# A decoder layer on one core: the last expert's down product in two other PSUM banks, the one hot vectors built in halves, and the last four tiles' accumulators added by TensorE with the unit matrix

## The reference

```python
for e in range(48):                      # gathered tokens of expert e, at most 192
    g, u = split(xb[e] @ gate_up[e].T)   # 192 x 512 by 512 x 384
    out[e] = (silu(g) * u) @ down[e].T   # 192 x 192 by 192 x 512
final = zeros(2048, 512)
final[token of the row] += weight of the row * out[e][row]
x = layernorm(x + final)
```

## Time and profile before

| | |
|---|---|
| time, median of 3 runs | 929.57 us (929.04 to 931.65) |
| time of the profiled execution | 927.28 us |
| its span, first to last instruction | 925.5 us |
| TensorE busy | 853.3 us, 92% of the span |
| VectorE, ScalarE, GpSimd busy | 651.3, 403.7 and 466.3 us |
| mean granted TensorE clock | 0.984 |

### The profile page before, as it was taken

How to read it: one execution, slowest core, us unless ns; L and a number is a source line. 1 busy time by engine, 2 the same in 40 slices (tenths; PEclk the granted TensorE clock), 3 DMA queues, 4 the chain that set the end, 5 groups by cost and what they waited for, 6 DMA issues and landing times.

```text
span 925.5 us, 18712 instructions
## 1 busy us (share of the span) xinstructions
PE 853.3 (92%) x6014; PEld 722.1 (78%) x6015; DVE 651.3 (70%) x1473; ACT 403.7 (44%) x825; POOL 466.3 (50%) x444
## 2 busy tenths in 40 slices
PE   6799999999999989999999689999999999999891
PEld 4577777777777777888888588988889889888770
DVE  6756766577656765777777886768767686667876
ACT  4332333322333322323322156756666666566623
POOL 0242233333343231555545547767767777678355
PEclk9999999999999999999999899999999999999996
DMA  9551111211121017233222399999999999997874
GB/s 337 186 207 47 47 47 58 78 45 45 45 87 39 24 56 229 74 109 107 88 94 87 118 268 294 288 288 292 289 289 291 296 297 302 255 251 137 222 222 159
DMA packets 72350, 154.98 MB, mean 167 GB/s; under 512 B 9888, under 2 KB 10544, under 8 KB 71920
## 3 DMA queue, kind: packets, MB, share of 16 engines
q1 hardware_dynamic: 50240, 99.81, 33.1%
q0 software_dynamic: 22064, 54.58, 23.8%
HBM read 110.29 MB, written 44.07 MB: 167 GB/s over the span
## 4 chain that ended last, share of the span: by engine, by line
PE 73%; DVE 13%; issue 7%; ACT 3%; DMA 1%; POOL 1%; DVEq 0%; another core or an unknown queue 0%; POOLq 0%; SPq 0%; ACTq 0%
PE ps L621 25%; PE ps L1002 19%; PE ps L1015 11%; PE ps L991 3%; PE ps L726 2%; PE ps L716 2%; DVE arena L1445 2%; PE ps L688 1%; DVE arena L1384 1%; DVE arena L1378 1%; PE ps L888 1%; DVE arena L1919 1%; PE ps L802 1%; ACT o_hi L1213 1%; ACT arena L1065 1%
## 5 line engine op out<-in xcount | busy, mean ns | idle before, releaser
L2079 POOL DMA_INDIRECT y_rows<-arena,place_token x92 | 151.0, 1641 | 79.7 <-issue 51.7
L2068 POOL DMA_INDIRECT xg<-x_rows,place_token x96 | 95.6, 995 | 36.8 <-issue 27.1
L1002 PE MATMUL ps<-arena,raw 128*128 128x192 f32 x576 | 99.8, 331 | 3.1 <-issue 3.1
L1002 PEld LDWEIGHTS ps<-arena,raw 128*128 128x128 f32 x576 | 95.8, 193 | 6.1 <-issue 4.0
L621 PE MATMUL ps<-w_hi,x_hi 128*128 128x512 f32 (+1 forms) x332 | 77.5, 355 | 10.0 <-ACT arena L1065 4.7
L1002 PE MATMUL ps<-arena,mid_flat 128*128 128x192 f32 x432 | 73.6, 327 | 2.6 <-DVE arena L1808 1.3
L1941 POOL TENSOR_TENSOR arena<-arena,attn_pack 128x512 f32<-128x512 f32 x12 | 16.0, 1337 | 118.7 <-DVE arena L1396 118.7
L1002 PEld LDWEIGHTS ps<-arena,mid_flat 128*128 128x128 f32 x432 | 70.7, 190 | 5.2 <-issue 2.8
L621 PE MATMUL ps<-w_hi,x_lo 128*128 128x512 f32 (+1 forms) x332 | 74.5, 346 | 0.0
L621 PE MATMUL ps<-w_lo,x_hi 128*128 128x512 f32 (+1 forms) x332 | 73.0, 342 | 0.0
L621 PEld LDWEIGHTS ps<-w_hi,x_hi 128*128 128x128 f32 x332 | 52.4, 189 | 22.3 <-issue 9.3
(11 more groups left out here) (259 smaller groups left out, 2055.1 us busy)
## 6 DMA issues: line engine op xcount, KB each, us to landing
raw<-in_gu SPq DMA_DIRECT2D x24, 768.0 KB
mid_flat<-in_gu SPq DMA_DIRECT2D x18, 768.0 KB
raw<-in_dn SPq DMA_DIRECT2D x24, 256.0 KB
y_rows<-zero SPq DMA_DIRECT2D x20, 256.0 KB
mid_flat<-in_dn SPq DMA_DIRECT2D x18, 256.0 KB
arena<-in_gu SPq DMA_DIRECT2D x6, 768.0 KB
arena<-in_xT SPq DMA_DIRECT2D x16, 256.0 KB, 3.0
x_res<-in_x SPq DMA_DIRECT2D x16, 256.0 KB, 2.8
```

The source lines that it names most:

```text
L1002: m = pe.matmul(out, wgu[slot][:, q, part * P:(part + 1) * P], xgT[:, p, q, :], start=(q == 0), stop=(q == KC - 1))
L2068: pool.indirect_dma_start(out=xg[:, place, h, :], out_offset=None, in_=x2_d, in_offset=bass.IndirectOffsetOnAxis(ap=place_token[:, 2 * n + ...
L2079: pool.indirect_dma_start(out=y2_d if p and n < DUAL else y_d, out_offset=bass.IndirectOffsetOnAxis(ap=place_token[:, 2 * n + h:2 * n + h ...
```

## The change

**Banks.** The down product of the last expert goes to the banks CT and CT + 1 (0 and 1) instead of CY and CY + 1 (4 and 5). It then waits for c_copied (the turned tokens have been read from the banks 0 and 1) instead of for y_scaled of the expert before. `KEPT_BANKS` is turned so that the tiles 6 and 7 take the banks 0 and 1; a wait for y_scaled[0] ahead of the first kept product guards 4 and 5.

**Halves.** `one_hot_tokens(block, half)` now builds 8 tiles with one instruction. Half 0 stands where the two stood. Half 1 stands one expert later, between the low parts of h and `scale_y`; that of block 2 stands behind `keep_rows(0)`.

**The last four tiles** (`SUMMED = NT - 4 = 12`, pieces 6 to 8). VectorE's add L1916 and GpSimd's add L2110 of these tiles are gone. TensorE adds y2 and y to the bank itself, by two fp32 products with the unit matrix (`sum_of_both`), and waits for the loads of y and y2 first. `bn_stats` and the scaling on ScalarE read the bank.

```diff
-        KEPT_BANKS = (0, 1, 2, 3, 6, 7, 4, 5)
+        KEPT_BANKS = (2, 3, 6, 7, 4, 5, 0, 1)
...
-            def c_down(p, k):
+            def c_down(p, k, bank=CY):
                 pe.wait_ge(dn_split[p], k + 1)
                 pe.wait_ge(h_split, 2 * k + p + 1)
-                at_least(pe, y_scaled[1 - p], 2 * (k + p))
+                if bank == CY:
+                    at_least(pe, y_scaled[1 - p], 2 * (k + p))
+                else:
+                    pe.wait_ge(c_copied, 2 * E2)
...
-                        m = pe.matmul(ps[0:HALF, CY + h, :], lhs, rhs, start=(i == 0), stop=(i == len(parts) - 1))
+                        m = pe.matmul(ps[0:HALF, bank + h, :], lhs, rhs, start=(i == 0), stop=(i == len(parts) - 1))
...
-            c_down(1, E2 // 2 - 1)
+            c_down(1, E2 // 2 - 1, CT)
...
-            pe.wait_ge(c_copied, 2 * E2)
+            def sum_of_both(j):
+
+                q = piece_of(j)
+                pe.wait_ge(y2_in[0], 4 * NT)
+                pe.wait_ge(y2_in[1], 4 * NT)
+                pe.wait_ge(y_in[q % 3], 16 * (q // 3 + 1))
+                pe.matmul(ps[:, KEPT_BANKS[j % 8], :], eye, y2_all[:, j, :], start=False, stop=False)
+                pe.matmul(ps[:, KEPT_BANKS[j % 8], :], eye, y_all[:, j, :], start=False, stop=True).then_inc(kept_made, 1)
+
             pe.wait_ge(h_made, 2 * E2)
             pe.wait_ge(place_made, NG + 1)
+            pe.wait_ge(y_scaled[0], E2)
...
-                kept_product(j, 1, stop=True).then_inc(kept_made, 1)
+                if j < SUMMED:
+                    kept_product(j, 1, stop=True).then_inc(kept_made, 1)
+                else:
+                    kept_product(j, 1)
+                    sum_of_both(j)
...
-                    m = act.activation(y_all[:, j, :], y_all[:, j, :], ACT.Identity, bias=shift3[:, j:j + 1], scale=rstd3[:, j:j + 1])
+                    row = y_all[:, j, :] if j < SUMMED else ps[:, KEPT_BANKS[j % 8], :]
+                    m = act.activation(y_all[:, j, :], row, ACT.Identity, bias=shift3[:, j:j + 1], scale=rstd3[:, j:j + 1])
...
+                if isinstance(n, int) and E2 - 3 <= n < E2 - 1:
+                    one_hot_tokens(n - (E2 - 3), 1)
                 if last:
                     keep_rows(0)
+                    one_hot_tokens(2, 1)
                 elif not first:
                     scale_y(1 - p, k - (1 - p))
...
-                    one_hot_tokens(n - (E2 - 4), p, k)
+                    dve.wait_ge(gu_made[p], k + 1)
+                    one_hot_tokens(n - (E2 - 4), 0)
...
-                else:
+                elif lo < SUMMED:
...
-                    m = dve.bn_stats(stat3[:, j, :], y_all[:, j, :])
+                    if j < SUMMED:
+                        m = dve.bn_stats(stat3[:, j, :], y_all[:, j, :])
+                    else:
+                        dve.wait_ge(kept_made, j + 1)
+                        m = dve.bn_stats(stat3[:, j, :], ps[:, KEPT_BANKS[j % 8], :])
...
-                if q + 1 < LAST:
+                if q + 1 < LAST and PIECES[q + 1][0] < SUMMED:
                     last_sum(q + 1)
```

More of the change, by code:

```diff
@@ L62 @@
 EARLY = 4
+SUMMED = NT - 4
 ARENA = 75 * 256
@@ L475, in experts, with piece_of @@
                 step(n, n % 2, n // 2, min(E2 - 1 - n, 2), n % RING, n // RING)
+        def piece_of(j):
+            return next(q for q, (lo, hi) in enumerate(PIECES) if lo <= j < hi)
         def before_it(p, k):
@@ L1272, in keep_rows @@
                 act.wait_ge(w_copied[p], E2 // 2)
-                act.activation(kept_y[0:HALF, 2 * p, :], ps[0:HALF, CY, :], ACT.Copy, scale=w_col[:, p, 0:1])
-                act.activation(kept_y[HALF:P, 2 * p, :], ps[P // 2:HALF, CY + 1, :], ACT.Copy, scale=w_col[P // 2:HALF, p, 1:2]).then_inc(y_scaled[p], 1)
+                bank = (CY, CT)[p]
+                act.activation(kept_y[0:HALF, 2 * p, :], ps[0:HALF, bank, :], ACT.Copy, scale=w_col[:, p, 0:1])
+                act.activation(kept_y[HALF:P, 2 * p, :], ps[P // 2:HALF, bank + 1, :], ACT.Copy, scale=w_col[P // 2:HALF, p, 1:2]).then_inc(y_scaled[p], 1)
                 act.wait_ge(y_scaled[p], E2)
@@ L1866, in kept_tokens, with one_hot_tokens @@
                 dve.wait_ge(tab_v, 6)
[L1868 to L1875, removed]
+            def one_hot_tokens(block, half):
+                js = slice(half * NT // 2, (half + 1) * NT // 2)
+                m = dve.tensor_tensor(hot_token[block][:, js, :], token_in_tile[:, block, js].unsqueeze(2).to_broadcast([P, NT // 2, P]),
+                                      rows[:, :].unsqueeze(1).to_broadcast([P, NT // 2, P]), ALU.is_equal)
+                if half:
+                    m.then_inc(hot_made, 1)
             def keep_rows(p):
@@ L1880, in keep_rows @@
                 dve.wait_ge(w_copied[p], E2 // 2)
-                dve.tensor_scalar(kept_y[p * P // 2:(p + 1) * P // 2, 1, :], ps[0:P // 2, CY + 1, :], w_col[0:P // 2, p, 1:2], None, ALU.mult)\
+                dve.tensor_scalar(kept_y[p * P // 2:(p + 1) * P // 2, 1, :], ps[0:P // 2, (CY, CT)[p] + 1, :], w_col[0:P // 2, p, 1:2], None, ALU.mult)\
                    .then_inc(y_scaled[p], 1)
```

## The result

| | before | changed |
|---|---|---|
| median of 13 runs | 929.16 us | 922.76 us |
| profiled execution, its span | 927.28, 925.5 us | 919.77, 918.0 us |
| TensorE busy | 853.3 us | 861.3 us |

The ratio is 0.9932, with a 95% interval of 0.991 to 0.9954: 6.4 us faster, where 4.1 was forecast. The runs of one kernel spread over 8 us before (923.25 to 931.65) and over 13 with the change (915.95 to 928.98), so one median says less than the profile does.

A forecast was written before the change was run, and what follows sets the result against it. TensorE was taken to bound the kernel up to the last experts, with VectorE and GpSimd holding each other in the layernorm. Terms 1.4 + 3.1 - 0.4 = 4.1 took the median 929.57 to 925.5; range 924.3 to 927.6.

The forecast's parts named there:

- halves, to the low parts of h: Experts 45 to 47: one half fewer ahead of the last low parts of h gains 0.8, bounds 0.5 and 1.18.
- banks, the wait for L1881: Last down product: it waits for h alone, no longer for L1881 emptying bank 5; gain 0.77.
- the last half: VectorE, between L1885 and the second L1881: the half now there delays L1881; cost 0 to 0.3, taken as 0.1.
- what the load of y lets through: GpSimd's first layernorm add waits for the first load of y; 1.4 of the 1.45 upstream gain passes.
- tiles, to `bn_stats` of 12, then of 15: Last four tiles on VectorE: adds and waits for GpSimd go, 1.30 + 1.46 + 0.37 = 3.1.
- What the end lets through: Behind the last tile: ScalarE's scaling and the stores close up; 0.4 taken off, bounds 0 and 1.2.
- rival (b): End of kernel: ScalarE and stores close up by 1.2, TensorE 0.5 late at tile 15; gain 2.8, chance 0.13.
- Rival (a): Layernorm start: scatters or first load of y come 1 later, 1.4 shrinks to 0.4; gain 3.1, chance 0.14.
- Rival (c): Last tiles: TensorE at the lower clock becomes the bound; slower, time 937, chance 0.05 in full or part.
- GpSimd's adds did hold VectorE's L1927: Layernorm piece 5: without GpSimd's adds L1927 takes 0.17 not 0.34; with tile 15's wait, 0.2 taken.
- The eight added fp32 products: TensorE, tiles 12 to 15: 0.90 each, 7.2 in all, hidden with 0.8 to spare or costing up to 0.3.
- `bn_stats` from a bank: VectorE, last four tiles: reading the bank costs 0 to 0.05 more each, taken as 0.

The follow-up runs named there:

- again: The changed kernel run again without edit; 61.85 from the mark (first one hot instruction of expert 44) to the end, ratio to the kernel before 0.9951.
- again3: The changed kernel run a fourth time without edit; 61.81 us from expert 44's first one hot instruction to the end, ratio to the kernel before 0.993.
- warm: The changed kernel with four small, never read fp32 products in TensorE's idle time ahead of the last down product; stretch 61.85, ratio to the kernel before 0.9944.
- again2: The changed kernel run a third time without edit; 63.00 us from expert 44's first one hot instruction to the end, ratio to the kernel before 0.9917.

## Why the forecast was right in kind, short in size and wrong about the end

| term | forecast | runs (again against before) |
|---|---|---|
| halves, to the low parts of h | 0.8 | 20.49 - 19.40 = 1.09 |
| banks, the wait for L1881 | 0.77 | 0.92 - 0.11 = 0.81 |
| the last half | -0.1 | -0.03 |
| what the load of y lets through | 1.4 of 1.45 | 1.83 of 1.87 |
| tiles, to `bn_stats` of 12, then of 15 | 1.47 + 1.66 | 1.51 + 1.70 |
| scaling, stores | -0.4 | +0.10, within the rounding of the spans |
| sum | 4.1 | 5.14, or 5.04 without the last term |

All of this is the stretch behind the mark at full clock.

**The step that failed** is the path behind the last tile, and with it the size of two terms. "What the end lets through ... I take 0.4 off" let the end of the span hang on ScalarE's scaling and the last store. It doesn't. These are the ends of the queues, from the last line of the program in again and then in the kernel before, with durations in ns and then the start in us:

```profile
L129 POOLq DRAIN  x1: 7537/7537/7537, 903.3 to 903.3; - x1
L129 ACTq EVENT_SEMAPHORE  x1: 17/17/17, 911.0 to 911.0; - x1
```

```profile
L128 POOLq DRAIN  x1: 7542/7542/7542, 917.7 to 917.7; - x1
```

GpSimd's queue ends with a DRAIN that begins together with its last instruction, the power L2118 of tile 15, and takes 7.54. The last semaphore instructions of the other engines come only behind it, at 911.0, which is the end of the span. It took 7.54 in 16 of the 18 profiles, and 7.4 in the two without the scatter. So the span ends 9.1 to 9.2 behind the start of `bn_stats` of tile 15 in both kernels (916.32 and 901.92), whatever ScalarE and the stores do.

And they did close up, as rival (b) had it. Six tiles came to ScalarE in a row; the last four took it 0.70 each from a bank, not the 0.76 by which I priced them, though the earlier trace rows had 0.69. ScalarE's timeline of again, against the earlier trace rows, and the last store of again, against the earlier trace rows:

```profile
900.84 1.52 ACT L1313 ACTIVATE arena<-arena 128x512 f32<-128x512 f32 x2 [0.36 <-DVE arena L1922]
902.38 2.78 ACT L1313 ACTIVATE arena<-ps,arena 128x512 f32<-128x512 f32 x4
```

```profile
out<-arena SPq DMA_DIRECT2D x1, 256.0 KB, 2.9
```

ScalarE ends at 905.16, 3.24 behind the start of `bn_stats` of tile 15; before it was 3.00 (919.32 - 916.32). The store lands 2.9 behind its issue and not 2.0. That is 1.1 more, near my upper bound of 1.2. But it lands at 908.1, 2.9 ahead of the end of the span, and the last store before at 921.4, 4.1 ahead of it. None of the 1.1 reached the time, so the term is nothing and not -0.4.

"Halves ... I take 0.8": the gain was 1.09, near the bound of 1.18 that VectorE alone sets. My walk had TensorE's starts right (again: 0.56 and 0.98 earlier at experts 46 and 47, where I had 0.6 and 0.95). But VectorE multiplies silu by up at expert 47 the whole 1.09 earlier, 16.77 behind the mark and not 17.86, and the low parts of h follow that, not TensorE's start.

"1.45 is about all that this load lets through" was half right. The load's issue scatters by itself, 23.6 to 26.9 behind the mark, because it hangs on the scatters. In the profile before it was late, 26.21, and I took that one value for the rule. In again, again3 and warm 1.8 to 1.9 came through, in again2 only 0.8. Rival (a) is a real mechanism that takes up to 1.1 in some executions.

**A term was missing.** The sum priced the idle time ahead of the last down product as 0.77 of waiting and put the clock behind it at nothing. In some executions the product then runs at the lower level. The profile before happened to show 1.00, the mean of the six unfilled profiles with the long idle time lost 0.74, that of the nine with the short one 0.13. If these shares held over many executions, that would be some 0.6 of gain beyond the 5.14. Three slow ones of six against one of nine are too few to show it. Rival (c) named the low clock, but at the last tiles, where TensorE works without a gap; there it stayed at 1.00.

**What took the time out of the range.** The sizes alone don't: 929.57 - 5.1 = 924.5, just inside the lower bound of 924.3. The measured time lies 1.7 below that. Of this 0.4 is luck of the base, the kernel before at 929.16 with 13 runs where it was 929.57 with three. The other 1.3 are the missing term of the clock and scatter, in shares that the runs don't split.

**What held.** GpSimd's adds did hold VectorE's L1927: with them gone, that of the same piece took 0.17 at 905.61, where before it took 0.34 at 909.90. The eight added fp32 products took 6.99 (TensorE ends 51.90 behind the mark instead of 46.78, and resumes 1.87 earlier), 0.87 each, below my 0.90. VectorE wanted tile 15 at 52.77, 0.87 later, as forecast 0.8. The last half costs nothing: the second L1881 starts 0.66 late and ends with ScalarE's pair. `bn_stats` from a bank took 0.69 as from SBUF. By VectorE: DVE Perf Modes in the Trainium skill, section on the TRN2 errata, a VectorE instruction has a fixed cost of 120 cycles from PSUM against 58 from SBUF. By that the four would have cost 0.26, an estimate from that page; the rows here don't bear it out.

**What stays open.** Whether anything ahead of the mark gained. The marks of ten profiles with the change of banks average 852.8, those of eight without it 853.9, on chips that differ, and one kernel alone spreads over 849 to 855 or 851 to 859. No instruction differs there, and the scatter covers it. The first measurement's 6.4 is 1.0 above the mean of the stretches, which is inside its interval. And what makes the clock fall behind the same idle time in one execution and not in the next: the runs don't show it.

## What to carry to other kernels

Ask what ends the span before pricing the last stage: here the scaling and the last store had 3 to 4 us to spare, and GpSimd's last instruction had none. Count a change from a mark ahead of which nothing differs, and take several profiles: behind the mark the same stretch came back to 0.05 us here while the whole moved by 9. A wait in front of TensorE can cost more than its length, because the product behind it can run at the lower clock level, and one profile can hide that. Where VectorE is the bound and TensorE is done early, adding by the unit matrix is worth it until TensorE is the bound. That came here between four tiles and six, at 1.75 of TensorE's time for each (6.99 / 4).

## What was not expected of the hardware

The DRAIN of GpSimd's queue took 7.54 us from its last instruction on and ended the span, 3 us or more behind the landing of the last store; what it waits for, no run shows. The lower clock level at a product of 2.53 was met in some executions and not in others of the same kernel, behind the same idle time of 2.75 (2.53, 3.40 and 4.09 in three profiles of the kernel before). And ScalarE took 0.70 for a tile from a bank where it takes 0.76 from SBUF, the same instruction with scale and bias.
